# A decoder layer in fp32r on one core: attention with batches outermost and unrolled, V computed token-major, row sums by transposes

## The chip, the cores and the metric

One core of one Trainium2 chip. The metric is the device time of the kernel in microseconds (us), lower is better. TensorE is called PE, VectorE DVE, ScalarE ACT, GpSimd POOL, and SyncE, which issues DMAs, SP.

## The reference, cut to what matters

```python
x = x + attention(layernorm(x))          # x: 4 batches x 512 tokens x 512, fp32
x = x + xattn(layernorm(x), token_ids)   # 4 experts, chosen by the token's id
x = x + ffn(layernorm(x))                # router, top 2 of 8 experts (352 wide), and a shared expert (704)

def attention(x):                        # 16 heads of 128
    q, k, v = split(x @ w_qkv)
    sim = tanh(q * SCALE @ k.T / 50) * 50
    attn = softmax(where(causal_mask, -max, sim))
    out = attn @ v * sigmoid(x @ w_gates)
    return concat_heads(out) @ w_out

def xattn(x, ids):                       # e = min(clip(ids, 0, 24999) // 6250, 3), W_e = ctx[e]
    return (silu(x @ W_e.T) * (x @ W_e.T)) @ W_e.T
```

## The kernel before, in words

Every product of two fp32 matrices is three matmuls in fp32r, hi by hi, hi by lo and lo by hi (`triple`, L278, with the matmuls in L279, L280 and L281). Each operand is therefore split: a copy rounds it to its high part (ACT, from PSUM or SBUF), and a subtraction makes the low part (DVE, or POOL for weights). Eight PSUM banks are given out by hand, the engines' programs are written out by hand with semaphores, and each engine works its instructions in order.

**Attention** is 64 units, one for each head and batch, with heads outer and batches inner: u = 4 h + b. Head 0 is written out; the others are a loop over h with four units in its body (PE, L1342; on ACT, DVE and POOL head 15 is written out too). The weights of q, k and v of a head are loaded together and split once per head, for four units. The normalized and transposed x (xnT_hi, xnT_lo) of all four batches stays in SBUF, 512 tokens wide. In a unit PE does, in this order (`head`, L1286):

- project q into bank 0 (12 matmuls of 512 columns), then output tile 0 of unit u-2 (3 matmuls, bank 7)
- project k into bank 1, then output tile 1
- project V into bank 0, as V transposed (a head's 128 features by 512 tokens), then output tile 2
- values of unit u-1 into bank 5 (12 matmuls of 128 to 512 columns), then the sums of its probabilities: two matmuls with a matrix of ones (`sum_probs`, L1270) over key_sums_hi and key_sums_lo
- output tile 3, the scores of unit u into banks 2 to 4 (12 matmuls), and four transposes of vT, which give V by tokens (L1338, bank 1)

ACT takes three tanh from the scores and one exp over 1280 columns (`softmax_part`, L609), then the high parts q_hi (L649), k_hi (L653), the copy vT (L664), o_hi (L624) and v_hi (L680). POOL multiplies by the causal mask (`mask`, L415), adds the probabilities over the four key tiles into key_sums (L424 to L428), splits these into hi and lo (L431, L434: four operations), and splits the weights (`low`, L394): three of wqkv and one of wo per head. DVE does, per unit: y_add of tile 0 (`y_add`, L892, adds an output tile times its factor to resid), q_lo, p_hi and p_lo of unit u-1 (`p_part`, L898), y_add of tile 1, k_lo, y_add of tile 2, o_lo, the factors from the sums (`y_factors`, L909: a transpose, four multiplications, a reciprocal), y_add of tile 3, v_lo.

The layer norm of batches 1 to 3, their transposes and gates stand in head 0, in units 0 to 2, as does the routing of tokens by their id (`route_x`, L860), in unit 3. After the last units the **tail**: the second layer norm of x needs all heads of a batch, and with heads outermost all four batches end in the last four units. Batch 0's norm is done in the last unit, batch 1's in the tail, those of batches 2 and 3 in the first steps of the next phase. Each normalized tile is scattered by POOL to a DRAM buffer in the order of the experts (`scatter_x`, L453). The ctx weights (ct, four matrices of 128 by 2048) are loaded and split at the end too: one on POOL, three on DVE (`ct_low`, L995).

Then come the **x phase** (22 tiles of 128 tokens of the id-routed experts), the router, the shared expert (16 tiles), the routed experts (39 tiles) and their combination. These phases are loops of steps of one shape. SP clears four DRAM buffers: two xs of 2.8 MB and es of 10 MB near the start, es_out of 10 MB after the heads' loads.

Of the kernel before, what the change touches and what calls it, by code (L numbers as in the profile page):

```python
# [5 lines left out]
F32 = mybir.dt.float32  # L6
F32R = mybir.dt.float32r
# [34 lines left out]
def build(nc, x, token_ids, wqkv, wgates, wo, ctxT, router, exp_up, exp_down, sh_up, sh_down, out):  # L42
    with ExitStack() as ctx:
# [28 lines left out]
        ones_r = sb("ones_r", [P, P], F32R)  # L72
# [45 lines left out]
        assert over_shared.at <= sb.at  # L118
        xT_hi = sb("xT_hi", [P, KC, P], F32R)
# [3 lines left out]
        aT_lo = sb("aT_lo", [P, SC, P], F32R)  # L123
        raw_at = sb.at
# [59 lines left out]

        ct_more = Region(sb.at)("ct_more", [P, 2 * KC * D])
        wqkv_raw = sb("wqkv_raw", [P, 3, KC, DH])
        wqkv_hi = sb("wqkv_hi", [P, 3, KC, DH], F32R)
        wqkv_lo = sb("wqkv_lo", [P, 3, KC, DH], F32R)
        wo_raw = sb("wo_raw", [P, D])
        wo_hi = sb("wo_hi", [P, D], F32R)  # L190
        wo_lo = sb("wo_lo", [P, D], F32R)
        gate_den = sb("gate_den", [P, TILES, HEADS])
        vT = sb("vT", [P, SEQ])
        key_sums = sb("key_sums", [P, SEQ])
        key_sums_hi = sb("key_sums_hi", [P, SEQ], F32R)
        key_sums_lo = sb("key_sums_lo", [P, SEQ], F32R)
        sums_T = sb("sums_T", [P, SEQ])
        denom = sb("denom", [P, TB])
        o_hi = sb("o_hi", [P, 2, SEQ], F32R)
        o_lo = sb("o_lo", [P, 2, SEQ], F32R)  # L200
        probs = sb("probs", [P, PCOLS])

        xrows = Region(sb.at)("xrows", [P, TB, D])
# [3 lines left out]
        gateT = sb("gateT", [P, SEQ])  # L207
        p_hi = sb("p_hi", [P, PCOLS], F32R)
        p_lo = sb("p_lo", [P, PCOLS], F32R)
        q_hi, q_lo, k_hi, k_lo, v_hi, v_lo = (sb(n, [P, SEQ], F32R) for n in ("q_hi", "q_lo", "k_hi", "k_lo", "v_hi", "v_lo"))  # L210
        factor = sb("factor", [P, 2, TB])
        assert sb.at <= raw_at
# [7 lines left out]
        names = """x_loaded0 x_loaded1 x_loaded2 x_loaded3 const_ready ones_ready ones_r_ready ln_stats ln_aggr ln_eps ln_rstd xn_ready xnT_ready xnT_hi_done xnT_lo_done  # L220
        wg_loaded  wg_split gateT_ready gateT_copied gate_ready gate_exp gate_done
        wqkv_loaded wo_loaded w_hi wq_split wk_split wv_split wo_split
        q_ready k_ready vT_ready v_ready s_ready pv_ready sum_ready y_ready
        q_hi_done k_hi_done vT_done v_hi_done o_hi_done tanh_done exp_done
        q_lo_done k_lo_done v_lo_done p_hi_done p_lo_done o_lo_done den_done sums_T_done factor_done y_added masked sums_step sums_done sums_hi_done sums_lo_done stored
        ids_loaded router_loaded zeros_ready zero_filled0 zero_filled1 zero_filled2 zero_filled3 step prefix_ready prefix_read prefix_e_read chosen_ready route_x_done route_e_done
        ct_loaded0 ct_loaded1 ct_loaded2 ct_loaded3 ct_hi_done ct_lo_pool ct_lo_dve sh_loaded sh_hi sh_split
# [63 lines left out]
        def _(sp):  # L291
            sp.dma_start(ids[:, :], token_ids).then_inc(S["ids_loaded"], 16)
            for b in range(BATCH):
                sp.dma_start(resid[:, TB * b:TB * b + TB, :], xv[:, TB * b:TB * b + TB, :]).then_inc(x_loaded[b], 16)
                if b == 0:
                    sp.dma_start(wg_raw[:, :, :], wgates).then_inc(S["wg_loaded"], 16)
                    sp.dma_start(wqkv_raw[:, :, :, :], wqkv[0]).then_inc(S["wqkv_loaded"], 16)
                    sp.dma_start(wo_raw[:, :], wo[0]).then_inc(S["wo_loaded"], 16)
# [3 lines left out]
            for n, (rows_of, tiles) in enumerate(((xs[0], XPART), (xs[1], XPART), (es, ETILES))):  # L302
                sp.dma_start(rows_of.rearrange("(t p) d -> p t d", p=P), zeros[:, :].unsqueeze(1).to_broadcast([P, tiles, D])).then_inc(S[f"zero_filled{n}"], 16)
# [1252 lines left out]
```

## Time and profile before

| | |
|---|---|
| median of 3 runs | 1809.78 us (1809.5 to 1814.93) |
| the profiled execution: span, first to last instruction | 1867.4 us |
| span less the median | 57.6 us |
| PE busy | 1726.2 us (92%) |
| PE weight loads busy (beside PE) | 1483.1 us (79%) |
| DVE busy | 964.8 us (52%) |
| POOL busy | 900.5 us (48%) |
| ACT busy | 577.4 us (31%) |
| mean granted clock of TensorE | 0.955 |
| DMA | 135.7 MB, mean 73 GB/s |

How to read it: the profiled execution is a run of its own, and its time is its span; no other time is on record for it. Busy time counts instructions at work, not those that wait. The span has four stretches: the start up to about 42 us, attention to 1062, the tail to 1097, and the later phases. Times of the rows are microseconds from the span's start. A bracket at a row's end is the engine's idle time before it and what ended it. The chain of waits follows the work that ended last back from release to release.

### The profile page before, as it was taken

The numbers are of one execution on the slowest core, as the hardware profiler recorded it, in microseconds if no ns is written. First come the engines' busy times: TensorE is split into PE (matmuls) and PEld (weight loads), VectorE is DVE, ScalarE is ACT, GpSimd is POOL, SyncE is SP. The second block draws the span as 40 slices with busy tenths as digits, with TensorE's granted clock in tenths as the row PEclk, the third lists the DMA queues.
The fourth block names the chain that finished last, engine by engine and source line by source line (L and its number), as shares of the span: only waits on it lengthen the run. The fifth ranks groups of instructions, "written<-read, shape, count | busy, mean of one in ns | idle before, by whom it ended". The sixth has DMA issues, their size and how long they took to land.

```text
span 1867.4 us, 27307 instructions
## 1 busy us (share of the span) xinstructions
PE 1726.2 (92%) x8800; PEld 1483.1 (79%) x8801; DVE 964.8 (52%) x1739; ACT 577.4 (31%) x1069; POOL 900.5 (48%) x823
## 2 busy tenths in 40 slices
PE   6989999999999999999999869998985999999881
PEld 4878888888888888888888658778974888999771
DVE  5766666666666666666666773344251222222225
ACT  3323333333333333333333413231110112333220
POOL 2546555655565556556555545510037006576404
PEclk9999999999999999999999979998796999999985
DMA  9300000000000000000025124420023005443425
GB/s 372 113 17 23 6 23 17 22 6 22 17 22 6 18 21 15 14 17 22 6 96 190 68 83 170 146 82 21 1 85 143 0 12 200 149 152 127 131 82 191
DMA packets 50913, 135.73 MB, mean 73 GB/s; under 512 B 5056, under 2 KB 5056, under 8 KB 48960
## 3 DMA queue, kind: packets, MB, share of 16 engines
q1 hardware_dynamic: 40464, 87.85, 13.3%
q0 software_dynamic: 10416, 47.46, 7.3%
q8 instruction: 18, 0.29, 0.1%
q14 instruction: 15, 0.12, 0.0%
HBM read 76.31 MB, written 58.98 MB: 72 GB/s over the span
## 4 chain that ended last, share of the span: by engine, by line
PE 87%; DVE 4%; another core or an unknown queue 3%; POOL 2%; issue 2%; DMA 1%; ACT 1%; DVEq 0%; ACTq 0%; POOLq 0%
PE bank L279 27%; PE bank L281 26%; PE bank L280 26%; PE bank L1398 2%; PE bank L1371 2%; PE bank L1338 1%; PE bank L1446 1%; PE bank L1275 1%; PE bank L1276 1%; DMA x_early<-es_out,slot_e 1%; POOL x_early L577 1%; DVE rows L780 0%; PE bank L1435 0%; DVE resid L895 0%
## 5 line engine op out<-in xcount | busy, mean ns | idle before, releaser
L279 PE MATMUL bank<-xnT_hi,wqkv_hi 128*128 128x512 f32 x768 | 307.9, 401 | 1.5 <-DVE xnT_lo L879 1.5
L281 PE MATMUL bank<-xnT_hi,wqkv_lo 128*128 128x512 f32 x768 | 302.5, 394 | 0.0
L280 PE MATMUL bank<-xnT_lo,wqkv_hi 128*128 128x512 f32 x768 | 300.5, 391 | 0.0
L895 DVE SCALAR_TENSOR_TENSOR resid<-bank,factor,resid 128x512 f32<-128x512 f32 x256 | 190.6, 746 | 201.6 <-PE bank L281 201.5
L419 POOL TENSOR_TENSOR probs<-probs,causal 128x256 f32<-128x256 f32 x128 | 92.0, 739 | 314.4 <-ACT probs L618 314.4
L1042 DVE TENSOR_TENSOR act_sb<-act_sb,bank 128x352 f32<-128x352 f32 (+1 forms) x93 | 50.6, 558 | 287.8 <-ACT act_sb L721 287.5
L279 PEld LDWEIGHTS bank<-xnT_hi,wqkv_hi 128*128 128x128 f32 x768 | 145.1, 189 | 32.7 <-issue 2.1
L281 PEld LDWEIGHTS bank<-xnT_hi,wqkv_lo 128*128 128x128 f32 x768 | 144.9, 189 | 32.1
L280 PEld LDWEIGHTS bank<-xnT_lo,wqkv_hi 128*128 128x128 f32 x768 | 145.3, 189 | 29.1
L721 ACT ACTIVATE act_sb<-bank 128x352 f32<-128x352 f32 (+1 forms) x93 | 44.5, 496 | 353.1 <-PE bank L281 287.8
L904 DVE TENSOR_TENSOR p_lo<-probs,p_hi 128x1280 fp32r<-128x1280 f32 x64 | 133.9, 2092 | 2.2
L1057 DVE TENSOR_TENSOR aT_lo<-bank,aT_hi 64x128 fp32r<-64x128 f32 (+3 forms) x148 | 56.6, 422 | 119.5 <-ACT aT_hi L712 116.2
L279 PE MATMUL bank<-wo_hi,o_hi 128*128 128x512 f32 x256 | 103.8, 405 | 10.3 <-DVE resid L895 5.2
L426 POOL TENSOR_TENSOR key_sums<-key_sums,probs 128x256 f32<-128x256 f32 x64 | 105.1, 1642 | 5.0
L279 PE MATMUL bank<-expert_w,xT_hi 128*128 x312 | 105.0, 336 | 2.4 <-DVE xT_lo L1026 2.4
L281 PE MATMUL bank<-wo_hi,o_lo 128*128 128x512 f32 x256 | 101.8, 398 | 0.0
L281 PE MATMUL bank<-expert_w,xT_lo 128*128 x312 | 101.6, 326 | 0.0
L280 PE MATMUL bank<-wo_lo,o_hi 128*128 128x512 f32 x256 | 101.5, 397 | 0.0
L280 PE MATMUL bank<-expert_w,xT_hi 128*128 x312 | 101.5, 325 | 0.0
L890 DVE TENSOR_TENSOR o_lo<-bank,o_hi 128x512 fp32r<-128x512 f32 x64 | 44.2, 691 | 108.8 <-ACT o_hi L624 108.7
L680 ACT ACTIVATE v_hi<-bank 128x512 fp32r<-128x512 f32 x64 | 38.2, 598 | 184.3 <-PE bank L1338 184.3
L424 POOL TENSOR_TENSOR key_sums<-probs 128x384 f32<-128x384 f32 x64 | 92.2, 1441 | 4.9
(256 smaller groups left out, 4345.5 us busy)
## 6 DMA issues: line engine op xcount, KB each, us to landing
wqkv_raw<-wqkv SPq DMA_DIRECT2D x16, 768.0 KB, 4.3
es<-zeros SPq DMA_DIRECT2D x1, 9984.0 KB, 41.1
es_out<-zeros SPq DMA_DIRECT2D x1, 9984.0 KB, 28.3
rows<-es SPq DMA_DIRECT2D x39, 256.0 KB
es_out<-rows SPq DMA_DIRECT2D x39, 256.0 KB, 2.0
xs<-zeros SPq DMA_DIRECT2D x2, 2816.0 KB, 20.6
rows<-xs SPq DMA_DIRECT2D x22, 256.0 KB
xs_out<-rows SPq DMA_DIRECT2D x22, 256.0 KB
```

What stands on the lines that cost most here:

```text
L279: nc.tensor.matmul(out_ap, a_hi, b_hi, start=first, stop=False)
L280: nc.tensor.matmul(out_ap, a_hi, b_lo, start=False, stop=False)
L281: return nc.tensor.matmul(out_ap, a_lo, b_hi, start=False, stop=last)
L419: nc.gpsimd.tensor_tensor(diagonal, diagonal, causal[:, :, :], ALU.mult).then_inc(S["masked"], 1)
L424: nc.gpsimd.tensor_tensor(key_sums[:, P:], probs[:, P:SEQ], probs[:, POFF[1]:POFF[1] + SEQ - P], ALU.add).then_inc(S["sums_step"], 1)
L426: nc.gpsimd.tensor_tensor(key_sums[:, 2 * P:], key_sums[:, 2 * P:], probs[:, POFF[2]:POFF[2] + 2 * P], ALU.add).then_inc(S["sums_step"], 1)
L721: nc.scalar.activation(act_sb[:, half * W:half * W + W], bank[2 * half][:, 0:W], ACT.Silu).then_inc(S[f"{ph}_silu"], 1)
L890: nc.vector.tensor_tensor(lo, ps, hi.bitcast(F32), ALU.subtract).then_inc(S[done], 1)
L895: nc.vector.scalar_tensor_tensor(out=row, in0=bank[of][:, :], scalar=factor[:, b % 2, i:i + 1], in1=row, op0=ALU.mult, op1=ALU.add).then_i ...
L904: nc.vector.tensor_tensor(p_lo[:, :], probs[:, :], p_hi[:, :].bitcast(F32), ALU.subtract).then_inc(S["p_lo_done"], 1)
L1042: nc.vector.tensor_tensor(part, part, bank[2 * i + (ph != "x")][:, 0:W], ALU.mult).then_inc(S[f"{ph}_act"], 1)
L1057: nc.vector.tensor_tensor(aT_lo[0:w, c0:c1, :], aT_bank(ph, c0, c1, w), aT_hi[0:w, c0:c1, :].bitcast(F32), ALU.subtract).then_inc(S[f"{ph} ...
```

## The change

1. The units are written out (no loops) with batches outer and heads inner, u = 16 b + h. q's, k's and wo's weights are therefore loaded and split in every unit (three high parts on ACT and three low parts on POOL per unit), V's per group of four units.
2. V is computed token-major: a tile of 128 tokens of xn is stationary, and the V weights of four heads (512 columns) move. One such `v_tile` is 12 matmuls and serves four heads. A table, V_SLOTS, places the four tiles of the next group in the units of this one: none in the first, tile 0 in the second, tile 1 in the third, tiles 2 and 3 in the fourth. Even tiles go to bank 0 and wait for q_lo, odd ones to bank 1 and wait for k_lo. The projection of V, the copy vT and the four transposes go. Group 0's four tiles stand at the start, and the last group computes none.
3. Row sums: key_sums is no longer split, and the two matmuls with ones go. PE transposes the four tiles of probs and key_sums into bank 6; DVE sums them with one reduction and makes the factors with one multiplication and a reciprocal.
4. The first layer norm of the next batch (LN_IN) stands in heads 5 to 8 of a batch's units, its transposes in heads 8 to 11, its gates in head 12. The second norm of the batch before (LN_X) and its scatter stand in heads 2 to 5. The routing by id stands in units 0 and 1. Only batch 3 is left for the x phase.
5. In a unit with V tiles output tile 2 comes after the first of them and tile 3 ahead of the scores; in one without, tile 2 comes after the sums and tile 3 after the scores. Scores wait for tanh, no longer for exp.
6. On DVE q_lo comes ahead of y_add 0, and k_lo ahead of y_add 1. The DRAM buffers are cleared in pieces of 1 MB, one per unit. ct 0 and 1 are loaded in unit 59 and split on POOL in units 61 and 62, ct 2 and 3 in the tail on DVE.

The core of the diff (sems and buffers aside):

```diff
+        V_SLOTS = {1: (0,), 2: (1,), 3: (2, 3)}
+        LN_X, LN_IN = 2, 5
@@ POOL, sum_keys and the units
-                pool.wait_ge(S["sums_done"], u + 1)
-                for source, to in ((probs, slice(0, P)), (key_sums, slice(P, SEQ))):
-                    nc.gpsimd.tensor_tensor(key_sums_hi[:, to], source[:, to], ones[:, 0:1].to_broadcast([P, to.stop - to.start]), ALU.mult).then_inc(S["sums_hi_done"], 1)
...
-            with pool.Fori(1, HEADS - 1) as h:
-                head(h, False, False)
+            for u in range(U):
+                b, h = divmod(u, HEADS)
+                if u:
+                    mask(u - 1)
+                if u % TB == 1 and TB * (u // TB + 1) < U:
+                    low_v(u // TB + 1, 2)
+                    low_v(u // TB + 1, 3)
+                if u:
+                    sum_keys(u - 1)
+                    low_wo(u - 1)
+                if u + 1 < U:
+                    low_q(u + 1)
+                if u % TB == 0 and TB * (u // TB + 1) < U:
+                    low_v(u // TB + 1, 0)
+                    low_v(u // TB + 1, 1)
+                if u + 1 < U:
+                    low_k(u + 1)
@@ DVE, y_factors and the units
-                nc.vector.transpose(sums_T[:, :], bank[6][:, :]).then_inc(S["sums_T_done"], 1)
+                nc.vector.tensor_reduce(denom[:, 0, :], bank[6][:, :].rearrange("p (t k) -> p t k", t=TB), mybir.AxisListType.X, ALU.add).then_inc(S["den_summed"], 1)
+                dve.wait_ge(S["den_summed"], u + 1)
+                nc.vector.tensor_tensor(denom[:, 1, :], denom[:, 0, :], gate_den[:, TB * b:TB * b + TB, h], ALU.mult).then_inc(S["den_done"], 1)
...
+                lo_part(q_lo[:, :], bank[0][:, :], q_hi[:, :], "q_hi_done", "q_lo_done", u)
+                if u >= 2:
+                    y_add(u - 2, 0)
+                if u:
+                    p_part(u - 1)
+                if u == 0:
+                    by_ids()
+                lo_part(k_lo[:, :], bank[1][:, :], k_hi[:, :], "k_hi_done", "k_lo_done", u)
@@ PE
+            def v_tile(n, to):
+                g, t = divmod(n, TB)
+                hi, lo = (a[:, :, t * P:t * P + P] for a in xnT[g // GROUPS % 2])
+                for k in range(KC):
+                    last = triple(to[:, :], hi[:, k, :], lo[:, k, :], wv_hi[:, k, :], wv_lo[:, k, :], k == 0, k == KC - 1)
+                last.then_inc(S["vt_ready"], 1)
...
-                nc.tensor.matmul(bank[6][:, :], ones_r[:, :], key_sums_hi[:, :], start=True, stop=False)
-                nc.tensor.matmul(bank[6][:, :], ones_r[:, :], key_sums_lo[:, :], start=False, stop=True).then_inc(S["sum_ready"], 1)
+                for i in range(TB):
+                    of = key_sums if i else probs
+                    last = nc.tensor.transpose(bank[6][:, i * P:i * P + P], of[:, i * P:i * P + P], ident[:, :])
+                last.then_inc(S["sum_ready"], 1)
...
-                    project(2, b, bank[0], "vT_ready")
...
-                        last = nc.tensor.transpose(bank[1][:, i * P:i * P + P], vT[:, i * P:i * P + P], ident[:, :])
...
+                for n in ahead:
+                    pe.wait_ge(S["k_lo_done" if n % 2 else "q_lo_done"], u + 1)
+                    v_tile(n, bank[n % 2])
+                    if n == ahead[0] and u >= 2:
+                        output_in_turn(u - 2, 2)
+                if u:
+                    values(u - 1)
+                    sum_probs(u - 1)
+                if not ahead and u >= 2:
+                    output_in_turn(u - 2, 2)
+                if ahead and u >= 2:
+                    output_in_turn(u - 2, 3)
+                scores(u)
+                if not ahead and u >= 2:
+                    output_in_turn(u - 2, 3)
```

How the order moves at three places. On PE, in a unit of the first kind (none of the V tiles), here is what stands between the k projection's end and the values. Before (the written-out head 0, with the gates' transposes that stand in it alone), the V projection starts there; its 12 matmuls, of which four are shown, and an output come before the values:

```order
L281 MATMUL bank<-xnT_hi,wqkv_lo 128x512
L279 MATMUL bank<-wo_hi,o_hi 128x512
L280 MATMUL bank<-wo_lo,o_hi 128x512
L281 MATMUL bank<-wo_hi,o_lo 128x512
L1234 MATMUL bank<-ident,gateT 128x128 x4
L279 MATMUL bank<-xnT_hi,wqkv_hi 128x512
L280 MATMUL bank<-xnT_lo,wqkv_hi 128x512
L281 MATMUL bank<-xnT_hi,wqkv_lo 128x512
L279 MATMUL bank<-xnT_hi,wqkv_hi 128x512
```

Now (store holds xn's high and low parts and V's, by slices):

```order
L303 MATMUL bank<-store,wqk_lo 128x512
L301 MATMUL bank<-wo_hi,o_hi 128x512
L302 MATMUL bank<-wo_lo,o_hi 128x512
L303 MATMUL bank<-wo_hi,o_lo 128x512
L301 MATMUL bank<-p_hi,store 128x512
L302 MATMUL bank<-p_lo,store 128x512
L303 MATMUL bank<-p_hi,store 128x512
```

The values follow output tile 1 directly. On DVE, in the units, before:

```order
L895 SCALAR_TENSOR_TENSOR resid<-bank,factor,resid 128x512
L890 TENSOR_TENSOR q_lo<-bank,q_hi 128x512
L902 CAST p_hi<-probs 128x1280
L904 TENSOR_TENSOR p_lo<-probs,p_hi 128x1280
L895 SCALAR_TENSOR_TENSOR resid<-bank,factor,resid 128x512
```

and now, in a unit with one V tile (its v_lo is the row that writes store):

```order
L933 TENSOR_TENSOR q_lo<-bank,q_hi 128x512
L939 SCALAR_TENSOR_TENSOR resid<-bank,factor,resid 128x512
L946 CAST p_hi<-probs 128x1280
L948 TENSOR_TENSOR p_lo<-probs,p_hi 128x1280
L933 TENSOR_TENSOR k_lo<-bank,k_hi 128x512
L939 SCALAR_TENSOR_TENSOR resid<-bank,factor,resid 128x512
L929 TENSOR_TENSOR store<-bank,store 128x512
L939 SCALAR_TENSOR_TENSOR resid<-bank,factor,resid 128x512
```

q_lo has moved ahead of the first y_add, k_lo to right behind p_lo, and v_lo is in the middle. On POOL, a unit before (weights are split here only in two of a head's four units):

```order
L419 TENSOR_TENSOR probs<-probs,causal 128x2x128
L419 TENSOR_TENSOR probs<-probs,causal 128x256
L424 TENSOR_TENSOR key_sums<-probs 128x384
L426 TENSOR_TENSOR key_sums<-key_sums,probs 128x256
L428 TENSOR_TENSOR key_sums<-key_sums,probs 128x128
L431 TENSOR_TENSOR key_sums_hi<-probs,ones 128x128
L431 TENSOR_TENSOR key_sums_hi<-key_sums,ones 128x384
L434 TENSOR_TENSOR key_sums_lo<-probs,key_sums_hi 128x128
L434 TENSOR_TENSOR key_sums_lo<-key_sums,key_sums_hi 128x384
```

and now, the second unit of a group:

```order
L464 TENSOR_TENSOR probs<-probs,causal 128x2x128
L464 TENSOR_TENSOR probs<-probs,causal 128x256
L426 TENSOR_TENSOR store<-wv_raw,store 128x512 x2
L470 TENSOR_TENSOR key_sums<-probs 128x384
L472 TENSOR_TENSOR key_sums<-key_sums,probs 128x256
L474 TENSOR_TENSOR key_sums<-key_sums,probs 128x128
L426 TENSOR_TENSOR wo_lo<-wo_raw,wo_hi 128x512
L426 TENSOR_TENSOR wqk_lo<-wqk_raw,wqk_hi 128x512 x2
```

The four splits of key_sums are gone, and two chunks of V's weights stand ahead of the sums, three other splits behind them.

## Rows read from the trace of the kernel before

**Rows 1.** The page: the chain that ended last, shares of the span.
```profile
PE 87%; DVE 4%; another core or an unknown queue 3%; POOL 2%; issue 2%; DMA 1%; ACT 1%; DVEq 0%; ACTq 0%; POOLq 0%
```

**Rows 2.** Windows: length; PE, PEld, DVE, ACT, POOL busy; clock; DMA.
```profile
122.00:1058.00 936.00, 935.62 (x4595) 790.00 (x4595) 598.02 (x947) 348.18 (x588) 542.27 (x588) 1.00 0.08 28
1062.20:1097.00 34.80, 14.52 (x46) 10.29 (x44) 31.61 (x40) 9.99 (x11) 24.94 (x19) 0.69 0.24 91
```

**Rows 3.** Timeline of PE, one unit: start, duration, line, operation.
```profile
502.80 0.44 PE L1275 MATMUL bank<-key_sums_hi,ones_r 128*128 128x512 f32 x1
...
503.31 0.39 PE L279 MATMUL bank<-wo_hi,o_hi 128*128 128x512 f32 x1
...
505.94 0.60 PE L1338 MATMUL bank<-ident,vT 128*128 128x128 f32 x4
506.29 0.48 PE L279 MATMUL bank<-xnT_hi,wqkv_hi 128*128 128x512 f32 x1
...
509.12 0.39 PE L279 MATMUL bank<-wo_hi,o_hi 128*128 128x512 f32 x1
...
512.56 0.39 PE L279 MATMUL bank<-wo_hi,o_hi 128*128 128x512 f32 x1
...
522.05 0.48 PE L279 MATMUL bank<-xnT_hi,wqkv_hi 128*128 128x512 f32 x1
```

**Rows 4.** Timeline of ACT: vT copies 59 units apart.
```profile
119.18 0.60 ACT L664 ACTIVATE vT<-bank 128x512 f32<-128x512 f32 x1 [2.84 <-PE bank L281]
...
1056.35 0.60 ACT L664 ACTIVATE vT<-bank 128x512 f32<-128x512 f32 x1 [2.84 <-PE bank L281]
```

**Rows 5.** Timelines of ACT, POOL and DVE after 506.29, the same unit.
```profile
507.07 1.36 ACT L616 ACTIVATE probs<-bank 128x512 f32<-128x512 f32 x3
508.46 1.27 ACT L618 ACTIVATE probs<-probs 128x1280 f32<-128x1280 f32 x1
509.64 0.58 ACT L649 ACTIVATE q_hi<-bank 128x512 fp32r<-128x512 f32 x1
...
509.81 1.44 POOL L419 TENSOR_TENSOR probs<-probs,causal 128x256 f32<-128x256 f32 x2 [7.65 <-ACT probs L618]
...
510.01 0.75 DVE L895 SCALAR_TENSOR_TENSOR resid<-bank,factor,resid 128x512 f32<-128x512 f32 x1 [2.12 <-PE bank L281]
510.68 0.68 DVE L890 TENSOR_TENSOR q_lo<-bank,q_hi 128x512 fp32r<-128x512 f32 x1
511.28 0.83 DVE L902 CAST p_hi<-probs 128x1280 fp32r<-128x1280 f32 x1
512.14 2.18 DVE L904 TENSOR_TENSOR p_lo<-probs,p_hi 128x1280 fp32r<-128x1280 f32 x1
```

**Rows 6.** Weight splits on POOL in the units: count, min/median/max ns.
```profile
L396 POOL TENSOR_TENSOR wqkv_lo<-wqkv_raw,wqkv_hi x42: 1288/1293/1299, 168.7 to 997.2; 128x512 fp32r<-128x512 f32 x42
```

**Rows 7.** Windows: the routing of tokens on DVE.
```profile
93.80:102.20 8.40, 4.96 (x26) 3.93 (x24) 7.78 (x20) 2.23 (x4) 4.54 (x4) 1.00 0.06 10
```

**Rows 8.** Timeline of PE: its first projection.
```profile
21.55 0.76 PE L279 MATMUL bank<-xnT_hi,wqkv_hi 128*128 128x512 f32 x1 [1.50 <-DVE xnT_lo L879]
...
26.80 0.61 PE L279 MATMUL bank<-xnT_hi,wg_hi 128*128 128x512 f32 x1
```

**Rows 9.** DVE and PE: a ct split, the next phase's first matmul.
```profile
1093.63 2.28 DVE L997 TENSOR_TENSOR xnT_lo<-ct_more,xnT_hi 128x2048 fp32r<-128x2048 f32 x1
...
1096.99 0.79 PE L279 MATMUL bank<-xnT_hi,xT_hi 128*128 x1 [5.37 <-DVE xT_lo L1026]
```

**Rows 10.** Timeline of PE: two matmuls after idle time.
```profile
39.37 0.47 PE L279 MATMUL bank<-q_hi,k_hi 128*128 128x512 f32 x1 [1.74 <-issue]
...
1246.57 0.49 PE L279 MATMUL bank<-xnT_hi,aT_hi 128*128 x1 [1.55 <-DVE aT_lo L1057]
```

**Rows 11.** Windows: around the first of them.
```profile
37.60:41.00 3.40, 1.66 (x11) 1.52 (x10) 1.29 (x2) 0.77 (x2) 0.00 (x0) 0.99 1.05 411
41.00:44.40 3.40, 3.40 (x14) 3.01 (x13) 0.95 (x2) 1.58 (x4) 0.00 (x0) 0.51 1.05 404
```

More of the change, by code:

```diff
@@ L206, in build @@
         wg_lo = sb("wg_lo", [P, KC, P], F32R)
[L207 to L212, printed above, removed]
+        gateT = wg_raw[:, :, :].rearrange("p k n -> p (k n)")
+        wv_raw = sb("wv_raw", [P, KC, D])
+        zeros = sb("zeros", [P, D])
+        assert sb.at <= nc.sbuf_usable_end
         xs = [nc.dram_tensor(f"xs{part}", (XPART * P, D), F32, kind="Internal").ap() for part in range(PARTS)]
@@ L310, in _ @@
[L310 to L320 removed]
+            for i in range(TB):
+                sp.dma_start(resid[:, i, :], xv[:, i, :]).then_inc(S[f"x_tile{i}"], 16)
@@ new lines, in _, with fill @@
+            sp.wait_ge(S["wk_split"], 1)
+            sp.dma_start(wqk_raw[:, :, :, :], wqk[1]).then_inc(S["wqk_loaded"], 16)
+            for b in range(1, BATCH):
+                sp.dma_start(resid[:, TB * b:TB * b + TB, :], xv[:, TB * b:TB * b + TB, :]).then_inc(S[f"x_loaded{b}"], 16)
+            sp.dma_start(router_w[:, :, :], router).then_inc(S["router_loaded"], 16)
+            def fill(rows_of, done, at, tiles):
+                sp.dma_start(rows_of.rearrange("(t p) d -> p t d", p=P)[:, at:at + tiles, :],
+                             zeros[:, :].unsqueeze(1).to_broadcast([P, tiles, D])).then_inc(S[done], 16)
@@ L1256, in scores, with values @@
                 last.then_inc(S["s_ready"], 1)
-            def values(u, first, sums=True):
+            def values(u):
                 pe.wait_ge(S["p_lo_done"], u + 1)
-                if not first:
+                pe.wait_ge(S["v_lo_done"], TB * (u // TB) + TB)
+                if u:
                     pe.wait_ge(S["o_lo_done"], u)
+                g, c = divmod(u, TB)
+                hi, lo = (a[:, :, c * DH:c * DH + DH] for a in v_of[g % 2])
                 for j in range(TB):
                     n = SEQ - P * j
-                    last = triple(bank[5][:, P * j:], v_hi[:, j * P:j * P + P], v_lo[:, j * P:j * P + P],
+                    last = triple(bank[5][:, P * j:], hi[:, j, :], lo[:, j, :],
@@ new lines, in output, with output_in_turn @@
+            def output(u, i, to=7):
+                pe.wait_ge(S["o_lo_done"], u + 1)
+                pe.wait_ge(S["wo_split"], u + 1)
+                triple(bank[to][:, :], o_hi[:, u % 2, i * P:i * P + P], o_lo[:, u % 2, i * P:i * P + P], wo_hi[:, u % 2, :], wo_lo[:, u % 2, :], True, True).then_inc(S["y_ready"], 1)
+            def output_in_turn(u, i):
+                if u == 0 and i == 0:
+                    pe.wait_ge(S["prefix_read"], 1)
+                if TB * u + i:
+                    pe.wait_ge(S["y_added"], TB * u + i)
+                output(u, i)
@@ new lines, in _ @@
+            pe.wait_ge(S["const_ready"], 3)
+            for t in range(TB):
+                transpose_xn(t, FIRST_BANKS[t])
+            pe.wait_ge(S["wv_split"], KC)
+            for n in range(TB):
+                pe.wait_ge(S["xnT_lo_done"], n + 1)
+                if n >= 2:
+                    pe.wait_ge(S["v_lo_done"], n - 1)
+                v_tile(n, bank[n % 2])
+            pe.wait_ge(S["wg_split"], 1)
+            gates(0)
+            transpose_gates(0)
+            pe.wait_ge(S["gate_exp"], 1)
```

882 lines of the change are left out of this document (429 added, 453 removed).

## The prediction, made before the changed kernel was run

> **What bounds the kernel now.** Begin with the table of engines: TensorE (PE) is busy 92% of the span, no other engine above 52%. The chain of waits agrees: 87% of it is PE, and 3%, some 56 us, lies with "another core or an unknown queue" [rows 1]. That is close to the 57.6 us by which the profiled span (1867.4) exceeds the median (1809.8), so I take it as something only the profiled execution shows. I sum changes against the profiled execution and apply the difference to the median. Next the table of windows: from 122 to 1058 us, the attention units, PE is busy 935.62 of 936.00 us at full clock. The 34.8 us after the last scores hold only 14.5 us of PE work, at a granted clock of 0.69 [rows 2]. So two places matter: in the units every matmul costs its time and every wait of PE is new time. In the tail after them PE waits already.
>
> PE's timeline shows one unit, 15.76 us long (506.29 to 522.05). Starts of successive groups give the pieces: from one output triple to the next, 509.12 to 512.56, fifteen matmuls of 512 columns take 3.44, so 0.229 each, 2.75 for a projection of 12 and 0.69 for an output triple; the pair of sum matmuls takes 0.51, four transposes 0.35 [rows 3]. Over 59 units the first and the last vT copy stand 937.17 us apart, 15.885 a unit [rows 4]; the 0.12 beyond 15.76 is what the loops add.
>
> **The change, part by part.**
> *Sums.* The pair (0.51) goes and four transposes of the sums come; the four of V go. Where a V tile is computed, a unit is 15.76 - 0.51 = 15.25 of PE work. The new code places the 60 V tiles after the first group unevenly (none, one, one and two in the four units of a group), so a unit without one is 15.25 - 2.75 = 12.50.
>
> *Unrolling.* The 0.12 a unit goes: 7 us, contained in these lengths.
>
> *The shorter unit meets the chain of the softmax.* Let T be the start of the q projection, just after the scores. Now the three tanh start only at T + 0.78 (507.07), behind v_hi, the split of the transposed V on ACT; that split goes, so tanh may start at about T + 0.2. They take 1.36, exp 1.27: T + 2.84. The mask takes 1.44, to T + 4.4 [rows 5]. But on DVE, p_hi stands behind q_lo and the first y_add (0.68 and 0.75). q_lo needs q_hi, which ACT makes after exp in 0.58, at about T + 3.45; so p_hi starts near T + 4.95, against T + 4.99 now. It takes 0.83 and p_lo 2.18: T + 8.0. Now no one waits for it, as PE has three projections and three outputs (10.3 us) ahead of the values. In a unit without a V tile it has two and two: 2 x 3.44 = 6.88. So values waits 8.0 - 6.88 = 1.15 us. There are 15 first units of groups and three at the end: 18 x 1.15 = 21 us.
>
> *The V tile in bank 1.* The third unit of a group computes an odd tile, which needs bank 1, free only when k_lo is done. The new DVE order has k_lo right behind p_lo: 8.0 + 0.68 = T + 8.7, where PE is ready at T + 6.88. The wait is 1.8, in 15 groups 27 us. Behind it PE's in-order queue holds the values, two outputs and the scores, so nothing can fill it. The second unit's tile is even (bank 0, q_lo at T + 4.2: free), and in the fourth the even one goes first. For both waits together I take 48 us; the lower bound is 0 (the chain a microsecond and a half earlier), the upper 75 (p_lo stretched by 0.8, as sharing with POOL could).
>
> *POOL.* One weight split is 1.29 us [rows 6]. Before, a group has four of these, now sixteen (q, k, wo per unit and wv's four chunks). POOL was busy 542 us in 59 units, 9.2 each: 7.9 beside the splits [rows 2]. The first unit of a group has five splits: at most 7.9 + 6.45 = 14.3, less the four sum operations that go. That fits in a group (64 us) but hardly in one unit; a late wq_split would hold PE. I take 0 here. Two 2048-column splits of ctx weights run in units 61 and 62, about 4 x 1.29 each; 3 us (0 to 10).
>
> *Batches inside units.* Three more gates of 12 matmuls, 3 x 2.75 = 8.2; twelve tiles of four transposes and three gate transposes, 15 x 0.35 = 5.3. The layer norms run on DVE, 64% busy (598 of 936) [rows 2]. The routing of tokens, 8.4 us on DVE [rows 7], moves from unit 3 to unit 1, where the next units' q_lo stands behind it; I take 5 us on PE (0 to 8.4).
>
> *Start.* PE's first projection starts at 21.55, waiting for the last tile of the norm; twelve matmuls at half clock take 5.25 [rows 8]. V needs only one tile, so PE starts near 18.9: four V tiles 5.25 + 3 x 2.75 = 13.5, gates 2.75, their copy and exp 1.7, q and k 5.5, the splits of k 1.3, scores 1.94: they end at 45.6 (before: near 41.7).
>
> *Sum to the last scores.* 45.6 + 63 x 12.50 - 2.76 (unit 1 has no outputs) + 60 x 2.75 + 48 + 8.2 + 5.3 + 5 + 3 = 1064.8. Now they end at 1062.2: **2.6 us later**. The 33 us of matmuls and 7 us of loops that go are eaten by the waits.
>
> *Tail.* Now the next phase's first matmul is at 1096.99, 34.8 after the scores; DVE had the norms and routing of a batch, ct splits (2.28 each) and the sums in between [rows 9]. Afterwards DVE has none of the norms: the wait and outputs 3.8, p_lo 4.2 later, values 3.5 at half clock, o_hi and o_lo 1.4, twelve matmuls at half clock 5.2, last y_add 0.75, one ct split 2.3, xT_lo 0.7 and 0.5 to PE: 22.4. So the phase starts at 1087.2, 9.8 us earlier. Later phases do the same work; fewer layer norms there don't lie on PE's path. Forecast: 1809.8 - 9.8 = **1800 us**; by its bounds, 1790 to 1815 (waits and tail rarely err in one direction).
>
> **The rivals.**
> *R1, the waits are not there.* If p_lo came by T + 6.9 nothing waits: 1800 - 48 = 1752. For it: mask could end 0.6 before p_hi starts. Against: q_hi behind exp and 3 us for p_hi and p_lo, all measured. Chance 0.12.
>
> *R2, slower: the clock falls with the gaps.* At 39.37 PE had been idle 1.74 us, after transposes [rows 10]; in the 3.4 us before 41.0 the granted clock was 0.99, in the next 3.4 us it was 0.51, that is 1.2 instead of 2.4 GHz, and PE was busy throughout [rows 11]. At 1246.57, after 1.55 us idle, the matmul took 0.49 [rows 10], where the cold one at 1096.99 took 0.79 [rows 9]: the clock held. The new gaps are 1.8 and 1.15. A fall costs 1.7 us of work (half of 3.4). If every gap of the third units does it, 15 x 1.7 = 26: 1826; if all 33 did, 56: 1856. It decides where gaps exceed some 1.6 us. Chance 0.20. The Trainium skill (TensorE: Matmul & The Clock Gate, section "A second HAM failure mode: psum-queue depth-cycling") says that short idles of PE between groups of matmuls make its clock swing between the two levels and cost throughput; by that rule the 1826 holds. The trace of before has one row for it and one against.
>
> *R3, slower: instruction fetching.* The loops become straight code, PE's rows in the program three times as many. If an engine waits for its instructions beside the fills, a third to all of the 56 us that the chain has now would be paid: 1819 to 1856. For it: the "unknown queue" entry. Against: it is not in the median. Chance 0.08. The Trainium skill (Runtime: NRT & Kernel Launch, section "Instruction fetch mechanics") says the reverse, that taken branches break the prefetch and straight code is hidden. Here loops cost 0.12 a unit, so the trace agrees in sign, and the rule gives no other sum.
>
> *R4, slower: POOL is the bound of a group.* If splits of q, k and wv come 2 us late in each group, 15 x 2 = 30: 1830. It decides where POOL's work in the first unit exceeds its 13.7 us (14.3 at most). Chance 0.10.
>
> **How the numbers follow.** A measurement here tells apart about 0.3%, 5.4 us: 1804.4 to 1815.2 is "same". The forecast (0.50) has its mass 0.34 below, 0.13 in, 0.03 above. R1 adds 0.12 to faster; R2, R3 and R4 add 0.01 to same and 0.37 to slower. So faster 0.46, same 0.14, slower 0.40. The range must leave out 0.2: the lower half of R1 and more, and the upper part of R2 and R3: 1770 to 1836. The likeliest case alone: 1790 to 1815.
>
> **What would show it.** In the changed profile: a group of four units about 64.0 us long (63.5 now); values waiting about 1.1 us for p_lo in first units; the odd V tile waiting 1.8 for k_lo in third units; no wait in the second and fourth; scores of unit 63 near 1065; the next phase 22 us behind. Granted clock at 1.00 in the units speaks against R2; PE waiting for wq_split, wk_split or wv_split is R4; waits with no named releaser are R3. I am wrong if PE waits for POOL in most units, or if groups are under 62 us (R1) or over 66.

## The result: 1.2% slower, and the profile after

The changed kernel takes 1831.97 us (median, 1828.2 to 1834.03) against 1812.03 us of the kernel before, measured beside it: ratio 1.0115, 95% interval 1.0091 to 1.0138. The forecast was 10 us faster; it is 20 us slower. The profiled execution of the changed kernel spans 1832.4 us, like its median; so the 57.6 us by which before's span exceeded its median belonged to that profiled execution, as the prediction took it. The later phases say the same: from their first matmul to the end they take 713.1 us now, and took 770.4 - 57.6 = 712.8.

The page of the changed kernel: span, engines, chain.

```profile
span 1832.4 us, 26328 instructions
...
PE 1691.5 (92%) x8672; PEld 1446.7 (79%) x8673; DVE 942.6 (51%) x1546; ACT 656.6 (36%) x1197; POOL 969.7 (53%) x759
...
PE 75%; DVE 10%; issue 6%; POOL 5%; ACT 2%; DMA 1%; SPq 0%; POOLq 0%; DVEq 0%; ACTq 0%
```

PE's busy time fell by 34.7 us, but its share of the chain fell from 87% to 75%: DVE and POOL have come onto the path. Who holds PE is in its waits from 45 to 1097 us, the attention units (what PE waited for: us in total, times, the longest); before, PE stood idle for 0.38 us from 122 to 1058 [rows 2].

```profile
PE bank L301 <- DVE k_lo L933: 25.1, 15, 1.8
PE bank L301 <- DVE p_lo L948: 13.2, 15, 1.1
PE bank L301 <- DVE resid L939: 13.1, 6, 6.2
PE bank L301 <- POOL store L426: 5.7, 4, 1.8
PE bank L1268 <- ACT wg_raw L664: 2.1, 3, 0.7
```

The windows of the third, fourth and first unit of an ordinary group, then of unit 21, of unit 2, and of the tail (length; PE, PEld, DVE, ACT and POOL busy; granted clock; DMA):

```profile
331.68:349.05 17.37, 15.57 (x79) 12.88 (x78) 10.61 (x16) 6.70 (x11) 8.97 (x8) 1.00 0.52 171
349.05:367.14 18.09, 18.09 (x91) 15.21 (x90) 11.25 (x22) 7.19 (x12) 10.03 (x9) 1.00 0.38 143
367.14:380.40 13.26, 12.14 (x64) 10.09 (x63) 8.02 (x10) 8.07 (x14) 9.91 (x9) 1.00 0.18 50
380.40:400.64 20.24, 18.16 (x82) 14.47 (x81) 16.48 (x22) 6.59 (x11) 15.22 (x14) 0.92 0.46 160
59.92:85.98 26.06, 18.59 (x79) 14.67 (x78) 18.72 (x39) 6.71 (x11) 7.67 (x9) 0.80 0.27 92
1096.67:1119.30 22.63, 13.76 (x50) 10.58 (x49) 16.70 (x21) 9.23 (x10) 8.64 (x6) 0.74 0.25 95
```

The edges of the units' windows are the starts of the last score matmul of each unit. A third unit idles 1.8 us, a first unit 1.1; together with the second (16.12) a group lasts 64.8 to 64.9 us. The windows of units 21 and 2 are the surprise. Unit 21, in which the second layer norm and the scatter of the batch before stand, lasts 20.24 (units 37 and 53: 21.02) where its like lasts 16.12, at a clock of 0.92; unit 2 lasts 26.06 at 0.80. The tail is 22.6 us, against 34.8 [rows 2]. It is shorter by 12 us, of which some 4 are the sums' (g_sums below).

Inside unit 21, the timelines of POOL and DVE:

```profile
383.67 1.22 POOL L479 DMA_INDIRECT xs<-xrows,slot_part  x1 [1.64 <-DVE xrows L836]
385.19 0.98 POOL L479 DMA_INDIRECT xs<-xrows,slot_part  x1 [0.30 <-issue]
386.19 1.44 POOL L464 TENSOR_TENSOR probs<-probs,causal 128x256 f32<-128x256 f32 x2
387.58 2.51 POOL L426 TENSOR_TENSOR store<-wv_raw,store 128x512 fp32r<-128x512 f32 x2
...
387.74 4.01 DVE L946 CAST p_hi<-probs 128x1280 fp32r<-128x1280 f32 x1 [1.57 <-POOL probs L464]
391.78 1.90 DVE L948 TENSOR_TENSOR p_lo<-probs,p_hi 128x1280 fp32r<-128x1280 f32 x1
393.60 0.68 DVE L933 TENSOR_TENSOR k_lo<-bank,k_hi 128x512 fp32r<-128x512 f32 x1
```

POOL waits for DVE's layer norm, issues two scatters, and only then masks the probabilities, exp of which ended at 383.45. p_hi, for which DVE stands idle 1.57 us, lasts 4.01 instead of 0.83 [rows 5] while POOL splits V's weights beside it. In the next stretch the clock is down:

```profile
390.40:393.80 3.40, 3.40 (x10) 2.59 (x10) 3.37 (x3) 0.00 (x0) 3.24 (x3) 0.53 0.00 0
```

Such falls last 3.41 us and come in units 21, 22, 37, 50 and 53, and one of 10.24 in unit 2: 27.3 us at 1.2 GHz, 13.6 us of work lost.

### The profile page after: what moved, and what is told of

It reads as the page before. It is cut to its first block, busy times and chain, and to the rows that moved or that the text cites. A ratio compares the mean times of both kernels' runs of the same rounds, so it can differ in the third digit from the quotient of the medians.

```text
span 1832.4 us, 26328 instructions
## 1 busy us (share of the span) xinstructions
PE 1691.5 (92%) x8672; PEld 1446.7 (79%) x8673; DVE 942.6 (51%) x1546; ACT 656.6 (36%) x1197; POOL 969.7 (53%) x759
## 3 DMA queue, kind: packets, MB, share of 16 engines
q1 hardware_dynamic: 56992, 138.20, 22.4%
## 4 chain that ended last, share of the span: by engine, by line
PE 75%; DVE 10%; issue 6%; POOL 5%; ACT 2%; DMA 1%; SPq 0%; POOLq 0%; DVEq 0%; ACTq 0%
PE bank L301 23%; PE bank L303 23%; PE bank L302 22%; DVE p_hi L946 3%; DVE p_lo L948 2%; PE bank L1448 2%; PE bank L1421 2%; PE bank L1315 1%; PE bank L1496 1%; POOL wqk_lo L426 1%; POOL probs L464 1%; DVE resid L939 1%; ACT q_hi L723 1%; POOL x_early L614 1%; DVE denom L960 1%
## 5 line engine op out<-in xcount | busy, mean ns | idle before, releaser
L301 PE MATMUL bank<-store,wqk_hi 128*128 128x512 f32 x512 | 202.0, 395 | 0.3 <-ACT gate_den L668 0.3
L303 PE MATMUL bank<-store,wqk_lo 128*128 128x512 f32 x512 | 202.1, 395 | 0.0
L302 PE MATMUL bank<-store,wqk_hi 128*128 128x512 f32 x512 | 201.9, 394 | 0.0
L426 POOL TENSOR_TENSOR wqk_lo<-wqk_raw,wqk_hi 128x512 fp32r<-128x512 f32 x128 | 163.1, 1290 | 14.4 <-ACT wqk_hi L629 14.4
L679 ACT ACTIVATE probs<-bank 128x512 f32<-128x512 f32 (+1 forms) x192 | 87.2, 528 | 156.6 <-PE bank L303 156.6
L933 DVE TENSOR_TENSOR q_lo<-bank,q_hi 128x512 fp32r<-128x512 f32 x64 | 44.3, 692 | 182.3 <-ACT q_hi L723 182.3
L301 PE MATMUL bank<-store 128*128 128x512 f32 x256 | 106.5, 416 | 30.8 <-DVE k_lo L933 25.1
L948 DVE TENSOR_TENSOR p_lo<-probs,p_hi 128x1280 fp32r<-128x1280 f32 x64 | 127.9, 1999 | 2.2
L303 PEld LDWEIGHTS bank<-store,wqk_lo 128*128 128x128 f32 x512 | 96.0, 188 | 23.2
L301 PEld LDWEIGHTS bank<-store,wqk_hi 128*128 128x128 f32 x512 | 96.0, 188 | 21.3 <-ACT gate_den L668 0.6
L302 PEld LDWEIGHTS bank<-store,wqk_hi 128*128 128x128 f32 x512 | 96.0, 188 | 21.3
L301 PE MATMUL bank<-expert_w,xT_hi 128*128 x312 | 103.7, 332 | 2.1 <-DVE xT_lo L1071 2.1
L303 PE MATMUL bank<-store 128*128 128x512 f32 x256 | 103.3, 403 | 0.0
L302 PE MATMUL bank<-store 128*128 128x512 f32 x256 | 102.7, 401 | 0.0
```

Of the source, the lines that this page charges most:

```text
L301: nc.tensor.matmul(out_ap, a_hi, b_hi, start=first, stop=False)
L302: nc.tensor.matmul(out_ap, a_hi, b_lo, start=False, stop=False)
L303: return nc.tensor.matmul(out_ap, a_lo, b_hi, start=False, stop=last)
L426: nc.gpsimd.tensor_tensor(lo, raw, hi.bitcast(F32), ALU.subtract).then_inc(S[done], 1)
L679: nc.scalar.activation(probs[:, lo:lo + n], bank[2 + i][:, 0:n], ACT.Tanh, scale=SCALE / SOFTCAP).then_inc(S["tanh_done"], 1)
L948: nc.vector.tensor_tensor(p_lo[:, :], probs[:, :], p_hi[:, :].bitcast(F32), ALU.subtract).then_inc(S["p_lo_done"], 1)
```

## Experiments

Two theories stood first. W: the cost is the two waits of every group, as predicted, and only their size or the clock was off. M: the cost beyond them is what the norms and the scatter of other batches, costed at nothing, do to the mask and to DVE. All medians below are of timed runs; before stood at 1810.1 to 1811.9 beside them.

**a_bank0: V tile 1 to bank 0.**

```diff
+        V_BANK = (0, 0, 0, 1)
-                    pe.wait_ge(S["k_lo_done" if n % 2 else "q_lo_done"], u + 1)
-                    v_tile(n, bank[n % 2])
+                    pe.wait_ge(S["k_lo_done" if V_BANK[n % TB] else "q_lo_done"], u + 1)
+                    v_tile(n, bank[V_BANK[n % TB]])
```

> The changed kernel with one edit: V tile 1, in the third unit of a group, goes to bank 0 and waits for q_lo, as tile 0 does, no longer to bank 1 behind k_lo (tile 3 alone keeps bank 1). Theory W (the wait for k_lo is as costly as its 25.1 us in 15 waits, and two of the five falls of TensorE's clock come from it): the 15 waits vanish, third units take 15.6 instead of 17.4, the falls in units 22 and 50 go (1.7 us each), so 25 to 29 us less: about 1805. Rival Q (the wait only moves: the values in the same unit then wait for p_lo, or the k projection of the next one for the bank): a new wait of 1 us or more stands in third units, and at most 10 us are gained: 1822 or more.

1800.68 us, ratio to before 0.9928 (0.9900 to 0.9955): 31 us less than the change. The waits of PE in the units:

```profile
PE bank L302 <- DVE resid L940: 14.6, 6, 6.2
PE bank L302 <- DVE p_lo L949: 13.2, 15, 1.1
PE bank L302 <- POOL store L427: 5.7, 4, 1.8
```

The row of k_lo is gone, nothing took its place, third units last 15.3 to 15.4 (15.8 where they hold transposes), and the falls of the clock in units 22 and 50 went with it. W holds for this wait, a little above its price. Two falls that the edit did not aim at went too, in units 37 and 53, which last 19.5 instead of 21.0 though PE still waits 1.8 and 1.0 us there (read in unit 37); unit 21 got longer, 21.8 instead of 20.2. So a few microseconds of the 31 lie where the falls happen to come. This one edit makes the kernel faster than before.

**b_spread: that, and one V tile in every unit up to 60.** Not shown: tile 3 goes to bank 0 too, and ACT makes the high parts of V's weights later in the first unit.

```diff
-            return [TB * (g + 1) + t for t in V_SLOTS.get(i, ())] if TB * (g + 1) < U else []
+            if i == 0:
+                return [TB * g + 3] if g else []
+            return [TB * (g + 1) + i - 1] if TB * (g + 1) < U else []
```

> As the kernel with V tile 1 in bank 0, and V tiles spread evenly: tiles 0, 1 and 2 of the next group in the second, third and fourth unit, tile 3 in the first unit of its own group, all in bank 0; every unit up to 60 has one V tile, so PE has 15.3 us of work in each. Theory W (values wait for p_lo only where a unit is short): the wait of 1.1 us (1.4 with its follow-up on resid) in the first unit of each group vanishes, 15 x 1.4 = 21 us less than the kernel with bank 0 alone: about 1784. Rival P (POOL, which has to split V's weights later in the first unit and the second, gets late): PE waits for the V weights' low part (store from POOL) in second units by 1 us or more, and 5 us or less are gained.

1781.37 us, ratio 0.9831 (0.9804 to 0.9858), 19 us less than a_bank0.

```profile
PE bank L304 <- DVE resid L942: 11.0, 4, 6.2
PE bank L304 <- POOL store L429: 7.1, 12, 1.7
PE bank L304 <- DVE p_lo L951: 1.7, 3, 1.1
```

p_lo is left in the three last units alone, which have no V tile: the wait was there because those units were short. Three units of four now last 15.33 to 15.38 with no wait, where the sum had 15.25. POOL's lateness of the rival exists too: second units wait 0.6 us for V's weights and still last 16.1, so an ordinary group gains only 0.7 us, not 1.4. That the total comes near the 21 expected is partly luck. Half of it, 9.8 us, lies in four units that theory W did not speak of, 2, 21, 37 and 53. Unit 37 in a_bank0 and in b_spread:

```profile
631.45:650.94 19.49, 16.63 (x82) 13.33 (x81) 16.54 (x22) 6.70 (x11) 15.09 (x14) 1.00 0.30 92
624.18:640.28 16.10, 15.61 (x78) 12.92 (x78) 12.64 (x19) 6.59 (x11) 13.77 (x12) 1.00 0.28 84
```

The norm and the scatter still stand where they stood, but behind a longer first unit the scatters start 0.7 us into unit 37, where the changed kernel has 2.6. So in units 37 and 53 their cost needs the short unit ahead of them; in unit 21 it stays (19.9).

**c_wvearly: POOL's splits of V's chunks 2 and 3 one unit earlier.**

```diff
-                if u % TB == 1 and TB * (u // TB + 1) < U:
-                    low_v(u // TB + 1, 2)
-                    low_v(u // TB + 1, 3)
...
+                if u % TB == 0 and TB * (u // TB + 1) < U:
+                    low_v(u // TB + 1, 2)
+                    low_v(u // TB + 1, 3)
```

> The changed kernel with one edit: POOL splits chunks 2 and 3 of V's weights at the end of the first unit of a group, no longer in the second between mask and key sums. It tells apart what makes units 21, 37 and 53 (with layer norm and scatter of the batch before) 4 to 5 us longer. Theory L (POOL's two splits hold DVE's p_hi, which took 4.01 us there, and V's weights come late): p_hi takes 1.6 or less, the waits for store (5.7 us in 4) vanish, the wait for resid of 1.84 and the fall of the clock behind it too; 3 x 4 + 2 = 10 to 14 us less: about 1820. Rival M (the mask is late because two scatters stand ahead of it on POOL, 2.3 us): p_lo stays late and only the 3 waits of 1.06 go: 1828.

1831.79 us, ratio 1.0110 (1.0085 to 1.0134): no gain. Of theory L only the smaller part is true: p_hi in unit 21 took 1.67 us, not 4.01, and the waits for POOL went, but the unit still lasts 19.1, for POOL now starts the mask at 388.53, still later. Elsewhere PE's waits for DVE grow; units 9, 25 and 41 last 18.3 instead of 16.5, which takes back what units 21, 37 and 53 gain:

```profile
PE bank L301 <- DVE k_lo L933: 25.1, 15, 1.8
PE bank L301 <- DVE resid L939: 21.3, 12, 6.3
PE bank L301 <- DVE p_lo L948: 13.2, 15, 1.1
```

**d_scatter: the scatter on POOL one unit later.**

```diff
-                if b and LN_X + 2 <= h < LN_X + 4:
+                if b and LN_X + 3 <= h < LN_X + 5:
...
-                    for i in range(2 * (h - LN_X - 2), 2 * (h - LN_X - 2) + 2):
+                    for i in range(2 * (h - LN_X - 3), 2 * (h - LN_X - 3) + 2):
```

> The changed kernel with one edit: the scatter of a normalized tile is issued on POOL at the end of the unit after the one in which DVE makes it, so that POOL no longer waits for DVE's layer norm ahead of the next mask. Theory M (the scatter makes the mask late): the mask of units 21, 37 and 53 ends 1.5 to 2 us earlier, these units lose most of their extra 4 to 5 us and the falls of the clock: 10 to 14 us less, about 1820. Rival L (the splits of V's weights hold p_hi): the units keep at least 3 us of their extra, 1828 or more.

1813.65 us, ratio 1.0018 (1.0002 to 1.0035), 18 us less than the change. Here are p_hi and what surrounds it in unit 21:

```profile
382.54 1.44 POOL L464 TENSOR_TENSOR probs<-probs,causal 128x256 f32<-128x256 f32 x2 [1.47 <-ACT probs L681]
383.93 3.15 POOL L426 TENSOR_TENSOR store<-wv_raw,store 128x512 fp32r<-128x512 f32 x2
...
385.10 0.82 DVE L946 CAST p_hi<-probs 128x1280 fp32r<-128x1280 f32 x1
385.95 2.48 DVE L948 TENSOR_TENSOR p_lo<-probs,p_hi 128x1280 fp32r<-128x1280 f32 x1
```

Units 21, 37 and 53 last 16.1 as their like, and their falls of the clock are gone. M is shown, and L falls as the main cause: the same two splits of weights stand beside p_hi here. What differs is who comes first. In unit 21 of the changed kernel p_hi has to wait for the late mask, behind which POOL begins its first split 0.15 us ahead of p_hi, and p_hi lasts until both splits and the addition behind them are over; here p_hi comes when the first split is at its end, takes 0.82 us, and the two splits take 3.15 instead of 2.51.

**e_route: the routing in four pieces.** The counting of tokens and the three parts of `route` stand in units 1 to 4, behind each unit's factors, no longer all in unit 1.

> The changed kernel with one edit: the routing of tokens on DVE (8.4 us in one piece in unit 1) is cut into four pieces, in units 1 to 4, each behind that unit's factors. Theory D (DVE's one piece makes PE wait 6.2 us for resid and lets its clock fall for 10.2 us): unit 2 takes 17.5 to 18 instead of 26.05 with no fall of the clock, and the kernel gets 8 us faster: 1824. Rival (the work is on DVE's path in any unit, so pieces only spread the wait): units 2 to 5 together lose less than 3 us.

1822.11 us, ratio 1.0067 (1.0045 to 1.0088), 10 us less than the change. Unit 2 lasts 18.96 instead of 26.05, with a short fall of 3.41 us left, and units 3 to 5 are longer by 0.4 in all. This is as expected, but for that fall: unit 2 was to take 17.5 to 18.

**g_sums: the sums alone, on the kernel before.** The edits of part 3, nothing else.

> The kernel before the change with part 3 of the change alone: row sums by four transposes of probs and key_sums, one reduction, one multiplication; no split of key_sums, no matmuls with ones. Heads stay outermost, loops and V as before. Theory: PE saves 0.51 - 0.38 = 0.13 us a unit, 8 us in all, and the tail saves 3 to 5 us of DVE's four small multiplications: 1810 - 12 = 1798. Rival (the transposes of fp32 data cost what the pair did, and nothing waits for DVE or POOL there): within 3 us of before.

1797.78 us, ratio 0.9936 (0.9920 to 0.9953): 12 us less. The group of four takes 63.10 us instead of 63.53, so 6.5 us in the loop's units; units 1 to 3 are 3.7 shorter, the tail from the last scores to the next phase is 31.3 instead of 35.0, and the start is 1.5 shorter. Together that is 15; the median fell by 12, and the difference lies in the later phases, which vary from run to run. This part of the change is a clean gain, and POOL has four operations less in each unit.

**f_best: b_spread, d_scatter and e_route together.**

> All edits that helped together: V tiles spread and in bank 0, the scatter a unit later, the routing in pieces. If the costs are independent: 1781 less 8 for unit 2 (23.5 to 15.4) less 4.5 for unit 21 (19.9 to 15.4): 1769, 2.3% below the kernel before the change. Rival: with no slack left on PE, pieces of DVE's and POOL's work show up as new waits: 1775 or more.

1762.50 us, ratio 0.9749 (0.9725 to 0.9772), 2.5% below before. The window of the units and PE's waits in them:

```profile
122.00:1030.00 908.00, 898.38 (x4447) 754.44 (x4446) 598.21 (x837) 418.57 (x704) 616.45 (x534) 1.00 0.29 97
```

```profile
PE bank L304 <- POOL store L429: 7.1, 12, 1.8
PE bank L304 <- DVE resid L953: 3.0, 2, 1.5
PE bank L304 <- DVE p_lo L962: 1.7, 3, 1.1
```

Units 2 and 21 last 15.35 and 16.15, the clock never falls before 1042, the tail is 20.1 us, and no new wait shows up. The units end 12 us earlier than in b_spread, as expected; the other 7 us of the 19 come behind the last scores and were not forecast. The gains do not add up over all runs: on the changed kernel d_scatter was worth 18 us, on b_spread it has only unit 21 left to mend, 3.8 us.

**h_wv, i_ct, j_both: three edits more on that.** h_wv has c_wvearly's edit; i_ct cuts the two ctx splits on POOL into four; j_both has both:

```diff
-                    nc.gpsimd.tensor_tensor(ct_lo[:, e], ct_raw(e), ct_hi[:, e].bitcast(F32), ALU.subtract).then_inc(S["ct_lo_pool"], 1)
+                    for k in range(KC):
+                        done = nc.gpsimd.tensor_tensor(ct_lo[:, e, k], ct_raw(e)[:, k], ct_hi[:, e, k].bitcast(F32), ALU.subtract)
+                    done.then_inc(S["ct_lo_pool"], 1)
```

> The combined kernel with chunks 2 and 3 of V's weights split on POOL at the end of the first unit, where the same edit gained nothing on the changed kernel. Theory P (second units wait for store from POOL, 7.1 us in 12 waits, and take 16.1 instead of 15.35 because the splits stand behind the mask there; with units evenly long POOL has room at the end of the first): second units take 15.4, 15 x 0.75 = 11 us less: 1751. Rival (as in the changed kernel, second units with nine or more heads done get longer since POOL is late with q's and k's splits): within 3 us of 1762.

1760.60 us, ratio 0.9716 (0.9693 to 0.9739). Mechanism right, size short: most second units last 15.35 and PE waits for POOL no more, yet those of heads 5 and 9 keep 16.0 to 16.4. The last scores end 7 us earlier than in f_best (1026.3 against 1033.4), but the phases after them took 5 us more in the profile, with longer falls of the clock; the median moves by 2, less than can be told apart.

> The combined kernel with the two ctx splits on POOL (2048 columns, 4.6 us each) cut into four of 512 columns. Theory O (a small operation of DVE, denom, waits until the POOL operation that has begun is over: it took 3.97 us in units 61 and 62 against 0.17): denom takes 1.3 us or less, units 62 and 63 take 13.3 instead of 14.95: 3 us less, 1759. Rival (DVE is locked out as long as POOL works, whatever the pieces): denom stays at 4 us and units at 14.9, no change.

1771.28 us, ratio 0.9756 (0.9721 to 0.9791), no gain. Theory O is right on DVE's operation, wrong on its worth. f_best's and i_ct's rows of denom and of the split beside it:

```profile
1003.63 3.97 DVE L974 TENSOR_TENSOR denom<-denom,gate_den 128x4 f32<-128x4 f32 x1
...
1002.97 4.61 POOL L514 TENSOR_TENSOR store<-raw,store 128x2048 fp32r<-128x2048 f32 x1 [0.64 <-ACT store L703]
```

```profile
1002.71 0.66 DVE L976 TENSOR_TENSOR denom<-denom,gate_den 128x4 f32<-128x4 f32 x1
...
1002.05 5.06 POOL L515 TENSOR_TENSOR store<-raw,store 128x512 fp32r<-128x512 f32 x4 [0.63 <-ACT store L705]
```

A DVE operation of 0.17 us stands still until the POOL operation that runs is over, 3.97 us or 0.66. But the pieces take POOL 5.06 instead of 4.61, PE then waits up to 2.0 us for p_lo, its clock falls at 1013, and unit 62 takes 16.4 instead of 14.95, unit 63 14.4.

> Both edits on the combined kernel. If they are independent: 1762 - 11 - 3 = 1748. If POOL has no room: 1756 or more.

1766.18 us, ratio 0.9736 (0.9707 to 0.9764): POOL has no room, as the rival had it. h_wv's gain in second units is there, but units 62 and 63 take 16.4 and 16.3, with a fall of the clock in each. f_best and h_wv are the best versions; 2 us between them can't be told apart.

## Why the prediction was wrong

By its own steps, with the trace of the changed kernel:

- *Start.* The first scores end at 45.31; forecast 45.6. Right.
- *Waits of a group.* 1.11 for p_lo in first units (forecast 1.15) and 1.81 for k_lo in third ones (1.8). Place and size right, and a_bank0 and b_spread show both to be causes. The pieces inside were not all right: in unit 20 p_hi took 1.36 us beside POOL's additions, not 0.83, and p_lo 1.91, not 2.18, so that the close hit has some luck in it.
- *Ctx splits.* Units 62 and 63 take 3.0 us more than unit 61 together; forecast 3. Right.
- *Tail.* 22.6 us; forecast 22.4. Right.
- *Sum to the last scores.* They end at 1096.67, forecast 1064.8: 32 us, and all of the error. Unit by unit against the sum it has these parts.
  - **First and largest, 14 us** (units 21, 37 and 53, 13.9 more than their like): "The layer norms run on DVE, 64% busy" costed the norm and scatter of the batch before at nothing. DVE had room in the mean; what was not asked is what stands behind POOL's wait. In POOL's in-order queue the scatter waits for DVE's norm, and the mask, p_hi, p_lo and k_lo wait behind it. d_scatter removes all 13.9. b_spread removes the 9.8 of units 37 and 53 too, without moving the scatter: there it takes both, the scatter's wait and the short unit ahead of it.
  - **Second, 13 us**: a group takes 64.9, not 63.95. The waits are as forecast; PE's busy time is 61.9 instead of 61.0. b_spread shows 0.1 us a unit of this to be matmul time: one V unit without any wait takes 15.33 to 15.38, not 15.25. The rest, 0.4 to 0.5 a group, goes in b_spread together with the waits. Some of it is seen behind each wait, where the second matmul starts 0.31 to 0.34 us after the first and not 0.23.
  - **Third, 4 us**: the routing took 9.0 in unit 2, not 5, as the clock fell for 10.24 us.
  - **Fourth, 3 us**: falls of the clock in two third units, 22 and 50, where the sum has none; a_bank0 removes both, d_scatter one.
  - **Fifth, 2 us**: unit 1 waits 1.8 us for V's weights.
  - The new gates and transposes cost 10.7 instead of 13.5, and the last four units 1 less than summed, which takes 4 back.
- *Loops.* The sum put 0.12 us a unit to them. Before, a group's first unit lasts 15.96 and its third 16.05, the others 15.76. The third stands in the middle of the loop's body, so its part isn't the loop's end, and no run separates what it is; both are gone in f_best.
- *R2, the clock.* Its mechanism is there, but seldom. It put a fall behind each gap of 1.8 us in third units, 26 us; of these fifteen gaps only two were followed by one, in units 22 and 50. The same fifteen gaps had one fall in d_scatter, three in c_wvearly and three in e_route. All falls of 3.41 us in the units of these four kernels begin 0.1 to 1.5 us after PE's return from a wait of 1.8 us, those in units 21, 37 and 53 too; but most waits of this length have none, and a_bank0 has one of 1.8 us and one of 1.0 in unit 37 at a clock of 1.00. So the length of the gap alone does not decide it, and the "some 1.6 us" of the prediction does not hold. With the long fall in unit 2, behind a wait of 6.2 us, it came to 13.6 us on top of the waits; that R2's 1826 lies near the measured 1832 is luck. The Trainium skill (TensorE: Matmul & The Clock Gate, "A second HAM failure mode: psum-queue depth-cycling") says that short idles between groups of matmuls make the clock swing. The trace agrees in kind; the forecast should have carried a share of it.
- *R3* did not show: none of PE's waits in the units is of unknown origin, the chain's "issue" (6%) lies in pieces of 0.5 to 1.0 us at handovers between engines where I looked (1060 to 1130 us), and "another core or an unknown queue" is gone from the chain. *R4*: POOL was late, but by its scatter; its weight splits cost 5.7 us in 4 waits, one in unit 1 and three behind the scatters. *R1*: no.

The range held the time (1770 to 1836); the likeliest case had the wrong sign.

## What to carry to other kernels

Costing work at nothing because an engine has room in the mean needs one more look: on each in-order engine that touches the moved step, its DMA issues included, write down what stands behind the step's wait, and follow that to the bound engine. When work is taken out of the bound engine's cycle, ask first which chain hides behind the cycle's length, and spread what is left evenly: one V tile a unit was worth 19 us, a bank that is free earlier 31 us, with no work removed. Half of the 19 came from units with other work in them, for which a short unit just ahead had been the trouble; so look at all units after an edit, not only at those that it aims at. A wait costs more than its length when the clock falls with it, and whether it falls is partly chance: an edit elsewhere moves the falls.

## What the runs showed of the hardware

- POOL and DVE keep each other waiting by whole operations, and who comes first decides which of them waits. DVE's 128 x 4 multiplication took 3.97 us beside one POOL subtraction of 4.61, and 0.66 beside four of 1.27. p_hi took 4.01 to 4.05 us in units 21, 37 and 53 of the changed kernel, where the first of two POOL splits had begun 0.15 us ahead of it, and outlasted both and the addition behind them; it took 0.82 in d_scatter, where it came at the end of the first split, and there the second split waited.
- Matmuls of the same shape start 0.232 us apart in the changed kernel's units and 0.230 in those of the kernel before and of g_sums, at full clock, mean of some 2800 pairs each. It is most of the 0.1 us a unit above. In the projections it is 0.233 against 0.229. No run was made to find its cause: layout of x in SBUF, the DMA traffic (94 against 28 GB/s) and straight code all changed, and it stays open. Straight code alone is unlikely, as the written-out start of the kernel before has 0.227 to 0.229.
- The same work after the last scores, tail included, took 727.5 us in the profile of f_best, 732.3 in that of h_wv and 739.8 in that of i_ct, and falls of the clock differ in these phases (a fall of 20.5 us in i_ct where f_best has 3.4). Edits of under 5 us can't be judged by the total here; by the time of the last scores they can.
